# The first 32 score steps of a head-dim-8 attention issued inside the last seven iterations of the attention ahead of it

## The reference, cut to what matters

```python
x = _layernorm(x + _L0_attn_ref(x, ...))
x = _layernorm(x + _L0_xattn_ref(ctx_1024, x, ...))      # 16 heads of 64, keys: 512 latents and 32 of the context
x = _layernorm(x + _L0_ffn_ref(x, ...))
# inside _L0_ffn_ref
q = (src @ Wq + bq).reshape(B, T, N_HEAD, HEAD_DIM)      # HEAD_DIM = 8
k = (src @ Wk + bk).reshape(B, T, N_HEAD, HEAD_DIM)
v = (src @ Wv + bv).reshape(B, T, N_HEAD, HEAD_DIM)
scores = jnp.einsum('bqhd,bkhd->bhqk', q, k) * scale
probs = jax.nn.softmax(scores, axis=-1)
attn = jnp.einsum('bhqk,bkhd->bqhd', probs, v).reshape(B, T, D_MODEL)
```

## Time and profile before

| | us |
|---|---|
| median of 3 runs | 1936.75 (1935.54 to 1939.33) |
| the profiled execution, its own time | 1938.96 |
| its span in the profile | 1937.0 |
| granted TensorE clock, mean over the span | 0.938 of full |
| TensorE busy | 1683.1 (87%) |
| VectorE busy | 1323.9 (68%) |
| ScalarE busy | 946.8 (49%) |
| GpSimd busy | 314.4 (16%) |

### The profile page before, as it was taken

How to read it: one execution, slowest core, us unless ns; L and a number is a source line. 1 busy time by engine, 2 the same in 40 slices (tenths; PEclk the granted TensorE clock), 3 DMA queues, 4 the chain that set the end, 5 groups by cost and what they waited for, 6 DMA issues and landing times.

```text
span 1937.0 us, 24861 instructions
## 1 busy us (share of the span) xinstructions
PE 1683.1 (87%) x8020; PEld 744.4 (38%) x8024; DVE 1323.9 (68%) x3117; ACT 946.8 (49%) x2042; POOL 314.4 (16%) x476
## 2 busy tenths in 40 slices
PE   6789999999999989999899675556877799979998
PEld 2344545545544422222344221222433355524443
DVE  7477767767767668886663699999477577733333
ACT  2556556656645516667433556332243166653333
POOL 0000000000001022210377000000012222104443
PEclk8999999999999979999999888777999699989999
DMA  4000000000001121230000000000100523000000
GB/s 188 1 1 1 1 1 1 1 1 1 1 1 47 25 74 34 51 100 2 1 1 0 1 1 1 1 1 1 65 0 18 127 73 73 3 1 1 1 0 22
DMA packets 19808, 44.62 MB, mean 23 GB/s; under 512 B 3872, under 2 KB 13024, under 8 KB 18912
## 3 DMA queue, kind: packets, MB, share of 16 engines
q1 hardware_dynamic: 18768, 41.46, 7.3%
q10 hardware_dynamic: 912, 1.57, 0.3%
HBM read 32.99 MB, written 9.44 MB: 22 GB/s over the span
## 4 chain that ended last, share of the span: by engine, by line
PE 71%; DVE 19%; ACT 4%; issue 4%; DMA 1%; POOL 1%; SPq 0%; ACTq 0%; POOLq 0%; another core or an unknown queue 0%; DVEq 0%
PE ps L554 8%; PE ps L520 7%; PE ps L532 6%; PE ps L927 5%; PE ps L907 5%; PE ps L953 5%; PE ps L489 3%; PE ps L1351 3%; PE ps L1352 3%; PE ps L1240 3%; PE ps L1359 3%; PE ps L1251 3%; DVE arena L1690 2%; PE ps L509 2%; DVE arena L1677 2%
## 5 line engine op out<-in xcount | busy, mean ns | idle before, releaser
L1092 DVE TENSOR_REDUCE stat<-ps 128x1 f32<-128x512 f32 (+3 forms) x512 | 279.1, 581 | 88.4 <-PE ps L931 51.7
L1012 ACT ACTIVATE arena<-ps 128x512 f32<-128x512 f32 (+3 forms) x512 | 246.8, 515 | 144.3 <-PE ps L953 74.4
L658 ACT ACTIVATE arena<-ps,stat 128x544 f32<-128x544 f32 x256 | 180.4, 709 | 227.3 <-DVE stat L700 227.3
L700 DVE TENSOR_REDUCE stat<-ps 128x1 f32<-128x544 f32 x256 | 173.5, 719 | 147.0 <-PE ps L520 146.1
L927 PE MATMUL ps<-arena 72*128 72x128 bf16 (+1 forms) x480 | 171.6, 365 | 19.3 <-DMA arena<-b_parts 15.7
L953 PE MATMUL ps<-arena 75*128 75x512 bf16 (+1 forms) x480 | 165.1, 348 | 8.2 <-ACT arena L1012 5.9
L520 PE MATMUL ps<-arena 64*128 64x272 f32 x1024 | 155.0, 422 | 12.1 <-ACT arena L658 10.4
L554 PE MATMUL ps<-arena 128*64 128x512 f32 (+1 forms) x640 | 158.0, 606 | 6.9 <-DVE arena L720 5.5
L666 ACT COPY arena<-ps 128x512 f32<-128x512 f32 x256 | 137.0, 593 | 14.0 <-PE ps L532 14.0
L532 PEld LDWEIGHTS ps<-wA_sb,arena 128*128 128x128 f32 x1024 | 114.0, 142 | 68.1 <-issue 67.3
L532 PE MATMUL ps<-wA_sb,arena 128*128 128x128 f32 x1024 | 138.5, 279 | 0.0
(11 more groups left out here) (319 smaller groups left out, 2846.4 us busy)
## 6 DMA issues: line engine op xcount, KB each, us to landing
arena<-b_parts SPq DMA_DIRECT2D x168, 96.0 KB
b_parts<-arena SPq DMA_DIRECT2D x64, 128.0 KB, 1.8
reg<-wM_dram SPq DMA_DIRECT2D x1, 3072.0 KB, 10.0
reg<-wB_dram SPq DMA_DIRECT2D x1, 2048.0 KB, 12.5
reg<-wM_dram SPq DMA_DIRECT2D x1, 2048.0 KB, 16.6
reg<-wD_dram SPq DMA_DIRECT2D x1, 1817.0 KB, 10.7
wF_sb<-wF_dram SPq DMA_DIRECT2D x1, 1476.0 KB, 20.2
reg<-b_parts SPq DMA_DIRECT2D x12, 96.0 KB
```

The lines of the kernel that those rows point to most:

```text
L658: e.activation(prob_of(P, r).rearrange("p (a k) -> p a k", a=2), score_banks(r), ACT.Exp, bias=x_neg[:, at_:at_ + 1], accum_out=x_sums[:, ...
L700: e.tensor_reduce(x_neg[:, n % 4:n % 4 + 1], score_banks(r), AX.XY, ALU.max, negate=True).then_inc(sem("max_done"), 1)
L1012: e.activation(p_t[:, m % 8, q0:T], ps[:, S1 + m % S2, q0:T], ACT.Exp).then_inc(exp_done, 1)
L1092: e.tensor_reduce(nm[:, G % 2, u // 4, u % 4:u % 4 + 1], ps[:, step % S1, 0:keys(u)], AX.X, ALU.max, negate=True).then_inc(max_done, 1)
```

## The change

Steps 0 to 31 of the first `narrow` leave that stage's functions (`head = 32`: its loops on TensorE and VectorE begin at step 32) and are issued from inside `b2_pe` and `b2_dve`, in iterations 128 to 134, in lots of 3, 5, 4, 5, 5, 4 and 6 steps (`HEAD`). In iterations 128 to 132 a lot stands behind the drain's own work; in 133 it stands on TensorE behind the last part of the value product and ahead of `out`, and in 134 three steps stand ahead of the second half of `out` and three behind. On VectorE the maxima of 134 stand ahead of `total`. Step 21 takes the turn of the first 16 maxima with it.

q and k of batch 1 move into iterations 130 and 131 (`HEAD_QK`), into accumulator bank 3, and are read into `scr_1`, a piece of the arena that the cross attention has left, instead of `dev`. GpSimd now sets the ones rows, splits q and k of batch 1 and then the first maxima, waits for the last value product and only then clears the value tiles. V of batch 0, the centring and the sum of squares of the last norm move to steps 33, 36 and 40 (`EXTRA`). SP waits for the last value product before it writes the ones rows of the second pack set, and before it reads the packs of batch 1.

The core of the diff (the functions `qk`, `qk_read`, `max_step`, `turn_step` only move out of the engines' functions, apart from what is shown):

```diff
+            head_steps = 32
+            HEAD = {XPAIRS: (0, 3), XPAIRS + 1: (3, 8), XPAIRS + 2: (8, 12), XPAIRS + 3: (12, 17), XPAIRS + 4: (17, 22),
+                    XPAIRS + 5: (22, 26), XPAIRS + 6: (26, 32)}
+            HEAD_QK = {XPAIRS + 2: 0, XPAIRS + 3: 1}
...
+            def head_pe(e, steps):
+                for step in steps:
+                    if step == 0:
+                        e.wait_ge(sem("exp_done"), 2 * XPAIRS)
+                    early_parts["pe"](e, step)
+
+            def head_qk_pe(e, j):
+                e.wait_ge(sem("exp_done"), 2 * XPAIRS)
+                early_parts["pe_qk"](e, 1, j)
...
                             pv((i - 9) // 4, (4,))
+                    if i == XPAIRS + 5:
+                        head_pe(e, range(*HEAD[i]))
+                    if i == XPAIRS + 6:
+                        head_pe(e, range(HEAD[i][0], HEAD[i][0] + 3))
                     if r == 2:
                         if out_at(i - 1) is not None:
                             out(out_at(i - 1), 1)
...
+                    if i in HEAD_QK:
+                        head_qk_pe(e, HEAD_QK[i])
+                    if i in HEAD and i != XPAIRS + 5:
+                        head_pe(e, range(HEAD[i][0] + (3 if i == XPAIRS + 6 else 0), HEAD[i][1]))
...
+                    if i == XPAIRS + 6:
+                        for step in range(*HEAD[i]):
+                            early_parts["dve"](e, step)
...
+                    if i in HEAD_QK:
+                        e.wait_ge(sem("pv_done"), XP - 1)
+                        early_parts["dve_qk"](e, 1, HEAD_QK[i])
+                    if i in HEAD and i < XPAIRS + 6:
+                        for step in range(*HEAD[i]):
+                            early_parts["dve"](e, step)
...
+                scr_1 = at_(0, 4 * T).rearrange("p (s t) -> p s t", s=4)
...
-            uses = [("m", B - 1, 0), ("s", B - 1, 0)] if early is not None else [("qk", 0, j) for j in range(NQ)]
+            EXTRA = {head + 1: ("v", 0, 0), head + 4: ("m", B - 1, 0), head + 8: ("s", B - 1, 0)} if early is not None else {}
...
+            mats = [wt[w] for w in ([wq, rope[0], wk, rope[1]] if rope else [wq, wk])]
+
+            def bank_of(b, j):
+                return 4 + j if b == 0 else 3 if b == 1 and early is not None else 7
+
+            def qk(e, b, j):
+                if b:
+                    e.wait_ge(*src_ready[b])
+                    if at7["qk", b, j] > 1:
+                        e.wait_ge(b7_read, at7["qk", b, j] - 1)
+                else:
+                    e.wait_ge(*src_ready[j])
+                e.matmul(ps[:, bank_of(b, j), :], mats[j], src[:, b, :], start=True, stop=True).then_inc(written, 1)
...
+            def score_step(e, step):
+                G, u = step // 16, step % 16
+                hg, h, q = G % 4, u // 4, u % 4
+                if u == 0:
+                    e.wait_ge(packed[G % 4], 16 * 6 * (batches_0 + G // 4 + 1))
...
+            def turn_step(e, step):
+                G, u = step // 16, step % 16
+                if u == 5 and 1 <= G <= NG:
+                    e.wait_ge(m_split, 4 * G)
+                    if G == 1 and early is not None:
+                        e.wait_ge(sem("ctx_probs"), XP)
+                    if G >= 2:
+                        e.wait_ge(m_copied, groups_0 + G - 1)
+                    for qt in range(4):
+                        i = e.matmul(ps[0:12, 6, qt * 128:qt * 128 + 128],
+                                     m_pad[:, (G - 1) % 2, qt].rearrange("p i h -> p (i h)"), ident_bf,
+                                     start=True, stop=True)
+                    i.then_inc(m_turned, 1)
+
+            def head_step(e, step):
+                score_step(e, step)
+                turn_step(e, step)
...
             def pe(e):
...
-                                     skip_group_check=True)
-                        if causal:
-                            i = e.matmul(ps[:, step % S1, q * 128:q * 128 + 128], wt_bf[:, 0:128], wt_bf[:, 128:256],
-                                         start=False, stop=True, skip_group_check=True)
-                        i.then_inc(score, 1)
-                    if early is not None and step == 0:
+                        score_step(e, step)
+                    extra = EXTRA.get(step)
+                    if extra and extra[0] == "m":
                         e.wait_ge(*b2_done)
+                        e.wait_ge(b7_read, at7[extra] - 1)
                         e.matmul(ps[:, 7, :], wt["centre"], x_aux[:, B - 1, :], start=True, stop=True).then_inc(written, 1)
-                    if early is not None and step == 2:
+                    if extra and extra[0] == "s":
                         e.wait_ge(f_squared, B)
-                        e.wait_ge(b7_read, 1)
...
+                            e.wait_ge(b7_read, at7["qk", 1, NQ - 1])
                         pack = (G2 // 4) % 2
                         q0 = k * 128 if causal else 0
...
-                    if G % 4 == 0 and G // 4 + 1 < B and u % 3 == 0 and 3 <= u < 3 + 3 * NQ:
-                        qk(G // 4 + 1, u // 3 - 1)
-                    if G % 4 == 0 and G // 4 < B and u == 15:
-                        b = G // 4
+                    turn_step(e, step)
+                    if qk_at(step):
+                        qk(e, *qk_at(step)[1:])
+                    if v_of(step) and v_of(step)[0] == "v":
+                        b = v_of(step)[1]
+                        if early is not None and b == 0:
+                            e.wait_ge(*b2_done)
...
+                    e.nop().then_inc(qk_ready, 1)
+
+            def max_step(e, step):
+                G, u = step // 16, step % 16
+                e.wait_ge(score, step + 1)
+                if u == 0 and G >= 2:
...
-                for step in range(STEPS):
+                for step in range(head, STEPS):
                     G, u = step // 16, step % 16
-                    if early is not None and step == 1:
-                        f_square(e, B - 1, written, 1, b7_read)
-                    if early is not None and step == 3:
+                    use = EXTRA.get(step - 1, " ")
+                    if use[0] == "m":
+                        f_square(e, B - 1, written, at7[use], b7_read, at7[use])
+                    if use[0] == "s":
                         f_scale(e, B - 1)
...
-                e.wait_ge(*src_ready[B - 1])
-                e.memset(ones_row, 1.0).then_inc(ones_set, 1)
-                e.memset(vv[:, 0, :, :, :], 0.0).then_inc(vv_set, 1)
-                e.memset(vv[:, 1, :, :, :], 0.0).then_inc(vv_set, 1)
-                e.wait_ge(vv_set, 3 * nth + 2)
-                e.memset(vv[:, :, :, :, HD:HD + 1].rearrange("p a k h n -> p (a k h) n"), 1.0).then_inc(vv_set, 1)
...
+                if early is None:
+                    e.wait_ge(*src_ready[B - 1])
+                else:
+                    e.wait_ge(sem("ctx_turned"), XPAIRS - 2)
+                e.memset(ones_row, 1.0).then_inc(ones_set, 1)
+                if early is not None:
+                    split(e, 1, (0, 1))
+                    split_max(0)
+                    e.wait_ge(sem("pv_done"), XP)
+                e.memset(vv[:, 0, :, :, :], 0.0).then_inc(vv_set, 1)
+                e.memset(vv[:, 1, :, :, :], 0.0).then_inc(vv_set, 1)
+                e.wait_ge(vv_set, 3 * nth + 2)
+                e.memset(vv[:, :, :, :, HD:HD + 1].rearrange("p a k h n -> p (a k h) n"), 1.0).then_inc(vv_set, 1)
...
-                    if 1 <= G <= NG:
+                    if (2 if early is not None else 1) <= G <= NG:
...
-                    if G % 4 < 2 and G // 4 + 1 < B:
+                    if G % 4 < 2 and G // 4 + 1 < B and 16 * G >= head:
                         split(e, G // 4 + 1, (G % 4,))
...
-                    if early is not None and b == 0:
-                        e.wait_ge(sem("pv_done"), 24)
+                    if early is not None and b < 2:
+                        e.wait_ge(sem("pv_done"), (24, XP)[b])
...
                         for a in range(2):
+                            if a and early is not None:
+                                e.wait_ge(sem("pv_done"), XP)
                             for hg in range(4):
                                 e.dma_start(k_pack[a][hg][ROWS:ROWS + 3, :, :],
...
-                early.append(split_0)
+                early.update(pool_split=split_0, pe_qk=qk, dve_qk=qk_read, dve=max_step, pe=head_step)
```

147 lines of the change are left out of this document (70 added, 77 removed).

## The result

Beside each other on one chip, 11 runs each, the kernel before took 1938.93 us (median, 1932.83 to 1947.6) and the changed one 1931.99 us (1926.64 to 1934.39): a ratio of 0.9961, 95% interval 0.9945 to 0.9978, 4 to 11 us off. A second comparison gave less, 0.9977 [0.996, 0.9993], medians 1935.54 and 1938.2. The forecast, 4.65 us off and 1932, stands between the two (6.9 and 2.7 us by medians), and faster was the right side. The profiled execution took 1930.61 us around a span of 1928.7 at a mean granted clock of 0.942. (One thing in the text ahead of the prediction is wrong: `narrow` is called twice, not three times, narrow(0) and narrow(1).)

The account below looks back on a forecast made before the run. It took VectorE's maxima, with TensorE queued behind them, to bound the seam. Step 48 7.35 us earlier at full clock, less 2.7 for a clock fall, gives 4.65 off the median 1936.75: 1932 us, range 1927 to 1938.

Parts of the forecast that it names:

- The bound: Seam between the two attentions: VectorE's maxima, 0.61 us each, with TensorE queued behind; steps 0 to 31 took 26.85 us.
- Scores 0 to 21: In the drain: last value product begins at 680.5 us, its second half follows score 16 at 686.0, scores end at 689.9.
- The turn's wait of 2.8 us: Behind score 21: TensorE stands from 689.9 to 692.7 us until GpSimd has split k, then the first maxima.
- rival (c): At the turn: GpSimd ready sooner, q's split perhaps from 679.5; 10.1 us off in all, 1926.7; chance 0.12.
- The clock: One fall in or just behind the turn's pause, 3 to 3.5 us at half clock, costing 2.7 us (bounds nothing and 5).
- rival (d): Pauses for maxima from 675.3 to 680.5 us bring the clock down until step 48; 8.7 us later, 1945.5; chance 0.06.
- no wait at the turn: Sign of being wrong: TensorE doesn't wait there for the maxima's split, forecast 2 to 3 us near 690; points to rival (c).
- half clock ahead of 690 us: Sign of being wrong, in the drain: granted clock 0.50 before 690 us; points to rival (d).
- Step 32: First step behind the drain, with both kinds of score: at 705.0 us instead of 713.8.
- Steps 32 to 47: Behind the seam, with V, centring and squares added: 17.3 us, 1.4 more than before though at full clock.
- The root's share: In steps 32 to 47: ScalarE's root, 0.70 and 0.64 us, queued ahead of exponential 8; TensorE loses some 1.5 us.
- The sum: Step 48 7.35 us earlier at full clock, less 2.7 for the clock: 4.65 off, 1932 us; chance 0.45.

Follow-up runs that it names:

- fill kernel: Changed kernel with spare f32 products, read by nobody, ahead of scores 11, 15, 16, 20, 21 and the turn; median 1933.14 us, ratio 0.9979 to the kernel before.
- late turn with fill: Changed kernel with spare products before scores 11, 15, 16, 20, 21 and the turn moved behind score 25; median 1933.76 us, ratio 0.9974 to before.
- after again: Changed kernel unchanged, measured a second time beside the kernel before; median 1935.54 us, ratio 0.9977.
- turn late: Changed kernel with the turn of the first maxima behind score 25 instead of score 21; median 1932.7 us, ratio 0.9993 to the kernel before.
- root late: Changed kernel with the last norm's squares and their root two steps later; median 1933.76 us, ratio 0.9968 to the kernel before.
- head of 16: Changed kernel with only steps 0 to 15 in the drain instead of 32 steps; median 1936.06 us, ratio 1.0004 to the kernel before.
- fill, root late: Changed kernel with spare products before scores 11, 15, 16, 20, 21 and the turn, and squares two steps later; median 1931.34 us, ratio 0.9959 to before.
- before, fill: Kernel before with a spare f32 product of 256 columns behind each of scores 3 to 31; median 1933.67 us, ratio 0.998 to the kernel before.
- all three: Changed kernel with spare products, turn behind score 25 and squares two steps later; medians 1925.85 and 1924.18 us, ratios 0.9928 and 0.9941 to before.

## Why the prediction was right, step by step

**The bound** (maxima and TensorE behind them): right. With the maxima taken into the drain the seam is shorter by what the order gives, 5.56 us at full clock.

**Scores 0 to 21**: the last value product begins at 679.25, forecast 680.5 less 0.98, so 0.3 off; the second half at 684.99, forecast 686.0 less 0.98, no difference. Laying the new order on old durations works to a few tenths as long as the clock is the same.

**The turn's wait of 2.8 us**: its cause was right, its size and its showing not. GpSimd took 6.17 us for the split (683.22 to 689.39) where batch 0's row gave 6.77. Each pair of subtractions took 2.26 us (687.13 is one), where batch 0's took 2.65 and 2.47. The wait is 1.7 us at full clock (fill kernel), and late turn with fill bought 1.37. In after itself it doesn't show: the second half of the value product ran at half clock, 1.64 us longer, and TensorE came to the turn 0.06 us after GpSimd had ended. A slower TensorE took the place of a wait. The forecast's rival (c), GpSimd sooner, was right that it is and wrong about the reason: the split of k did not begin ahead of its read (683.22, the read ended at 683.10). It was also wrong about who would profit. Why the subtractions are shorter here was not tested.

**The clock**: I had one fall of 3 to 3.5 us, near 690 to 700, put down to the turn's wait, at 2.7 us. There were two, some 10 us together, and the first came ahead of the turn, behind the pauses of 1.10 and 1.11 us for maxima: the mechanism of rival (d), some 5 us later than (d) had it. That TensorE's idle time there is needed for it is shown: four traces of the unfilled order (after, after again, turn late, root late) have the fall, and in all five traces with spare products the value product behind them takes 1.94 us. That the two pauses suffice is not, since the head of 16 has both and no fall there. It came back within some 3 us, behind the dense half of a value product, so (d)'s price of 10.4 never came. The two falls made the two slow rows 4.1 us longer (1.64 and 2.48), and the first lay over the wait for GpSimd, so the whole price, after less fill, is 2.56 us. **That this is near the forecast's 2.7 is luck**: the falls were three times as long as forecast, and what they cost under the wait had been counted as the wait. Two of the forecast's own signs of being wrong came up, no wait at the turn and half clock ahead of 690 us, and only the run with spare products could tell how the parts add up. On the Trainium skill's rule that the throttled state is the default ("TensorE: Matmul & The Clock Gate", "What's actually happening"), the runs agree: the clock fell in a drain that had held it before waits were put into it.

**Step 32** at full clock was to come 35.2 us behind the start; the fill kernel has 33.67. Of the 1.5 us, 1.0 is gained at the turn (21.88 us behind the start, forecast 22.88), the rest between it and step 32. **Steps 32 to 47** were to take 17.3 us; they took 17.0. The root's share (1.5 forecast) measured 1.44, both as an idle and by the run that moved it. At 717.15 it holds an exponential, ScalarE's queue, as the prediction had it.

**The sum**: 4.65 us off; the seam gave 6.6. Step 48 was to come 55.18 us behind the start and came at 53.22. Of the 1.96 us, 1.66 are gained by step 32 and 0.3 in steps 32 to 47. Against the fill kernel, 1.5 of the 1.66 is the path at full clock, and the clock's price has only the other 0.14 (2.7 less 2.56). So the wait for GpSimd is the term that was mis-sized, 2.8 where 1.7 was measured; and it was added to the clock's price as a wait of its own, where in the kernel after half clock took its place. The median moved 6.9 us in one comparison and 2.7 in the other. That spread isn't the seam's, whose length was the same to 0.13 us in both executions of after.

**The spread** goes with the clock elsewhere. In the table, the tail (from 1377 us on in the kernel before) has the same work in each kernel and lasts from 552.5 to 563.0 us, in step with the time at half clock. TensorE in it, two windows of "fill, root late":

```profile
1500.00:1520.00 20.00, 17.88 (x59) 0.50 0.34 77
1520.00:1540.00 20.00, 19.67 (x119) 0.60 0.61 158
```

The same two of "head of 16":

```profile
1500.00:1520.00 20.00, 10.94 (x33) 0.50 0.58 130
1520.00:1540.00 20.00, 17.96 (x130) 0.92 0.41 112
```

So all timed spans can be held against their mean clock. Over the 80 executions of before beside the experiments it was 0.9386 on average, over 22 of after 0.9410. A common slope of 1.22 us for each 0.001 of clock, fitted over all kernels, puts them at a clock of 0.940 to:

```
                     executions  mean span  mean clock  span at 0.940
before                   80       1936.5     0.9386       1934.8
after                    22       1931.0     0.9410       1932.2
head of 16               10       1934.9     0.9400       1934.9
turn late                 9       1933.8     0.9397       1933.4
fill                     10       1930.5     0.9423       1933.3
fill, turn late          10       1932.1     0.9410       1933.3
root late                10       1931.3     0.9404       1931.8
fill, root late          10       1928.8     0.9423       1931.6
before, fill             10       1931.6     0.9451       1937.8
all three                18       1924.7     0.9440       1929.6
```

The kernel after is 5.5 us shorter by mean spans, 2.6 at the same clock and 2.9 by a better one; a value of the last column is uncertain by 0.2 (before) to 0.5 us (ten executions). "Before, fill" is longer at the same clock and shorter in all. But the two aren't quite apart: what a kernel gains of clock at the seam lifts its mean clock too, so the last column undervalues it. From 0.79 to 0.91 over 56 us, before to after, is 0.0035 in the mean of such a span by my estimate, more than the 0.0024 between the two, so after's better clock need not come from any other place. Why the stretch near 1500 us is short in one execution and long in another stays open: the seam's edits shift when the program comes there, but I tried nothing at that place.

## What to carry to other kernels

Work that an idle engine could do can be drawn into the dense drain of the stage ahead. Lay the new order on the old durations, look for who is queued behind the first thing that waits, and write down where each engine stands at each step. Cutting dense TensorE work into pieces can have a price in the clock that is larger than the wait one worries about (2.56 and 1.7 us here). A few spare products in the pauses tell which it is; by themselves they did not show in the timed runs. Count from the last common point ahead of the change, since the last part of the span moved by up to 10 us without the change. And a forecast that lands can do so with its parts wrong: read the waits, not only the time.

## What the runs showed of the hardware

The granted clock fell to 1.2 GHz near 685 us in after, with TensorE busy for 1.70 us of 2 (684 to 686) and for 0.89 of the two ahead of them, behind two pauses of 1.1 us that ended 5.1 us apart. The same two pauses brought no fall in the head of 16. In that kernel, 12 us with TensorE busy for 11.69 stood at 0.50 throughout, the first ten of them bf16 products alone, scores of 72 and 75 rows and a turn. In after each return came in or right behind eight f32 products of 512 columns in a row. That isn't what it takes, since in all three again it came behind V (products of 128 columns), scores, the centring (two f32 products of 512 columns) and a turn:

```profile
702.00:704.00 2.00, 2.00 (x10) 0.52 0.76 180
704.00:708.00 4.00, 4.00 (x9) 0.50 0.80 190
708.00:709.00 1.00, 1.00 (x6) 0.55 0.73 168
709.00:710.00 1.00, 1.00 (x8) 1.00 0.81 189
```

The fall at 685 us cost 1.64, the one near 924 in the kernel with the late root 1.7; a fall of some 3 us over dense work thus costs about half its length. Products that nobody reads, 5.7 us of them, kept the clock whole across the seam in both kernels that had them ahead of the turn too (fill; fill with the late root). In the three executions without those (and with the late turn) it fell again between 694 and 715 us.
